# A metaformer of four blocks on one core: another order in attention and triangle, shorter batch statistics, and half of a scan's centring ahead of a verdict

## The reference, cut to what matters

```
x = x + L0_conv(_ln_c(x))      # linear attention: softmax(q), softmax(k), context = k^T v
t = t + L0_ffn(_ln_t(t))       # spectral filters (STU): a causal convolution over 256 tokens
x = x + L1_conv(_ln_c(x))      # triangle: a, b = sigmoid products of x; z = a * b; g * (ln(z) Wz + bz)
t = t + L1_ffn(_ln_t(t))       # recurrence with batch statistics of Wx
x = x + L2_conv(_ln_c(x))      # scan over 16 image rows: row + relu(conv(previous row))
t = t + L2_ffn(_ln_t(t))       # 16 experts, top 8 tokens each
x = x + L3_conv(_ln_c(x))      # the same scan again, with other weights
t = t + L3_ffn(_ln_t(t))       # the same recurrence again

# L1_ffn and L3_ffn
mean, var = jnp.mean(flat, axis=0), jnp.var(flat, axis=0)     # flat = W x, over all 32 * 256 tokens
Wx = (flat - mean) * rsqrt(var + 1e-5) * gamma + beta
y[t] = sigmoid(Wx[t] + y[t-1] @ V.T)                           # 256 steps
```

## Time and profile before

| | |
|---|---|
| median of 3 runs | 474.16 us (472.72 to 477.4) |
| profiled execution | 474.01 us, span 471.9 us |
| TensorE busy | 424.3 us (90%), 2880 matmul passes |
| VectorE busy | 246.3 us (52%) |
| ScalarE busy | 181.3 us (38%) |
| GpSimd busy | 32.9 us (7%) |
| granted TensorE clock, mean | 0.975 |

### The profile page before, as it was taken

The page is one execution under the profiler, slowest core; times in us unless marked ns, Lnnn a source line. Parts: engine busy times, 40 slices in busy tenths (PEclk is TensorE's granted clock), DMA queues, the critical chain, the costliest instruction groups (busy, mean ns, idle before and its releaser), DMA issues.

```text
span 471.9 us, 7130 instructions
## 1 busy us (share of the span) xinstructions
PE 424.3 (90%) x2880; PEld 260.1 (55%) x2880; DVE 246.3 (52%) x486; ACT 181.3 (38%) x373; POOL 32.9 (7%) x39
## 2 busy tenths in 40 slices
PE   6967999999879999998999999897999899999990
PEld 2434656554255567653765555394475474475590
DVE  3499677786778050106103746646534628434735
ACT  1776777755530002001102643454504631414360
POOL 0037222222000000000000000000000000000000
PEclk8898999999999999999999999998999999999997
DMA  9940000079940000000002000000000000000003
GB/s 222 135 97 1 1 1 1 2 160 219 203 90 0 1 0 0 1 0 0 1 0 47 0 1 3 0 1 2 0 1 2 2 0 1 0 1 1 0 1 90
DMA packets 6479, 15.24 MB, mean 32 GB/s; under 512 B 2718, under 2 KB 5422, under 8 KB 5806
## 3 DMA queue, kind: packets, MB, share of 16 engines
q1 hardware_dynamic: 5870, 14.25, 14.9%
q10 hardware_dynamic: 576, 0.52, 0.3%
HBM read 5.86 MB, written 1.05 MB: 15 GB/s over the span
## 4 chain that ended last, share of the span: by engine, by line
PE 66%; DVE 17%; ACT 10%; issue 3%; DMA 1%; POOL 1%; POOLq 0%; SPq 0%; DVEq 0%; ACTq 0%
PE bank L673 20%; PE bank L532 17%; PE bank L213 6%; PE bank L861 5%; PE bank L207 4%; PE bank L806 4%; PE bank L817 3%; PE bank L229 2%; ACT lnv L272 2%; ACT rs L277 2%; DVE xn L259 1%; DVE xQ L1294 1%; DMA xR<-in_x 1%; PE bank L605 1%; ACT arena L1019 1%
## 5 line engine op out<-in xcount | busy, mean ns | idle before, releaser
L673 PE MATMUL bank<-xn,arena 128*128 128x512 f32 (+15 forms) x332 | 88.9, 427 | 2.4 <-DVE xn L259 2.4
L673 PEld LDWEIGHTS bank<-xn,arena 128*128 128x128 f32 x332 | 56.3, 190 | 36.0 <-issue 27.0
L266 ACT ACTIVATE sq<-bank 128x512 f32<-128x512 f32 x36 | 21.3, 591 | 118.0 <-PE bank L207 98.3
L532 PE MATMUL bank<-sb_consts 128*128 128x512 f32 (+1 forms) x116 | 52.9, 569 | 1.6 <-ACT arena L1153 1.6
L532 PE MATMUL bank<-xn,sb_w_attn 128*128 128x512 f32 x64 | 35.4, 644 | 4.8 <-ACT attn_scratch L990 3.7
L213 PE MATMUL bank<-sq,sb_consts 128*128 128x512 f32 x72 | 38.7, 623 | 0.7
L272 ACT ACTIVATE lnv<-bank 128x512 f32<-128x512 f32 x36 | 21.5, 597 | 35.4 <-PE bank L213 35.3
L1303 DVE TENSOR_TENSOR arena<-bank,rs 128x512 f32<-128x512 f32 x4 | 4.2, 1038 | 51.4 <-ACT rs L277 51.4
L532 PEld LDWEIGHTS bank<-sb_consts 128*128 128x128 f32 x116 | 20.5, 194 | 18.7 <-issue 16.5
L861 PEld LDWEIGHTS bank<-arena,sb_w_late 128*128 128x128 f32 x180 | 23.0, 191 | 11.1 <-DVE arena L1470 8.0
L861 PE MATMUL bank<-arena,sb_w_late 128*128 128x128 f32 x180 | 27.2, 287 | 1.7 <-DVE arena L1470 1.3
(11 more groups left out here) (193 smaller groups left out, 623.5 us busy)
## 6 DMA issues: line engine op xcount, KB each, us to landing
arena<-arena SPq DMA_DIRECT2D x4, 1024.0 KB, 16.0
arena<-arena SPq DMA_DIRECT2D x4, 512.0 KB, 8.7
arena<-in_w_spec SPq DMA_DIRECT2D x2, 720.0 KB
sb_w_late<-in_w_late SPq DMA_DIRECT2D x1, 1100.5 KB, 22.8
xR<-in_x SPq DMA_DIRECT2D x4, 256.0 KB, 4.5
arena<-arena SPq DMA_DIRECT2D x4, 256.0 KB, 4.1
sb_w_attn<-in_w_attn SPq DMA_DIRECT2D x1, 641.0 KB, 7.4
arena<-in_w_spec SPq DMA_DIRECT2D x2, 256.0 KB
```

What stands on the lines that cost most here:

```text
L266: act.activation(sq[:, i % 2, :], bank[:, centre_bank(i), :], ACT.Square).then_inc(S("ln_squared"), 1)
L532: return mm(ps, lhsT, rhs, start=True, stop=True)
L673: return mm(bank[:, k, lo * B:hi * B], lhs, cols[:, at * B:(at + hi - lo) * B], start=start, stop=stop, **kw)
```

## The change

It has four parts, and all of the diff is in them.

1. Attention: on TensorE the query product, the first filter and the value products of a turn move behind the transposes of the unit before (`attn_q_v`). On ScalarE a turn now begins with the query exponential and the key copy of the unit before, then the key exponentials, then the copy of the first filter; the query exponential of a unit thus moves to the next turn.
2. Triangle: the a-product's slices are given out in fours between the last steps of the spectral stage (`a_columns`), three of four in place of filler products; VectorE adds the bias to the first half of them ahead of the last normalisation; ScalarE makes two of its three scaled copies ahead of the sigmoids of b; the two numbers of fillers go from 3 and 4 to 2 and 2.
3. Batch statistics: two one-column operations are folded into their neighbours, one copy leaves the path, and one copy goes, ScalarE reading the bank itself. The shift of the scaling is now formed with the other sign.
4. First scan: `ln_centre_r` takes a set of residues. For quarters 0 and 1 the products r = 2, 3 run inside `rnn(0)`, the first two behind the sixth early state and ahead of the verdict's product, the second two in place of a filler; the products r = 0, 1 follow at the scan's start and wait for the eighth state instead of for GpSimd's release. Bank 3 takes the verdict's sum instead of bank 0.

The core of the diff:

```diff
-BUSY_ATTN, BUSY_TRI, BUSY_SCAN, BUSY_LOGITS = 4, (3, 4, 6, 1), 3, 2
+BUSY_ATTN, BUSY_TRI, BUSY_SCAN, BUSY_LOGITS = 4, (2, 2, 6, 1), 3, 2
-ACT_BD = 3
+ACT_BD, ACT_BD_FIRST = 3, 2
+LATE_R = (2, 3)
...
-                for m in filter_turn(u, 0):
-                    filters(m)
+
+            def attn_q_v(u):
+                j, q = divmod(u, NQ)
                 if u >= 1:
                     pe.wait_ge(S("q_shift"), u)
                 full(bank[:, 2, :], wq[:, q, :], flat(xn, j)).then_inc(S("q_ps"), 1)
+                for m in filter_turn(u, 0):
+                    filters(m)
...
                 if 0 <= i - 1 < U:
                     attn_mid(i - 1)
+                if i < U:
+                    attn_q_v(i)
...
-            keep_busy(BUSY_STU, 6)
+            def a_columns(ms):
+                for m in ms:
+                    pe.wait_ge(S("ln_applied"), 3 * CH + m // 4 + 1)
+                    last = full(bank[:, m // 4, (m % 4) * P:(m % 4 + 1) * P],
+                                xnH[:, m, :, :].rearrange("p g w -> p (g w)"), wa)
+                    if m % 8 == 7:
+                        last.then_inc(S("ab_ps"), 1)
...
-                pe.wait_ge(S("bn_v"), i + 1)
+                pe.wait_ge(S("bn_rstd"), i + 1)
...
+                if i == 0:
+                    pe.wait_ge(S("x_early"), RES - 2)
+                    ln_centre_r(pe, CH * (k + 1), xsQ, LATE_R)
                 pe.wait_ge(S("settled_rows"), i + 1)
-                full(bank[0:1, 0, 0:1], moved[:, 1:2], ones[:, 0:1]).then_inc(S("settled_sum"), 1)
+                full(bank[0:1, 3, 0:1], moved[:, 1:2], ones[:, 0:1]).then_inc(S("settled_sum"), 1)
                 if i == 0:
-                    keep_busy(BUSY[5], 4)
+                    ln_centre_r(pe, CH * (k + 1) + 1, xsQ, LATE_R)
...
-                    ln_pe_r(pe, k, xsQ, lambda: pe.wait_ge(S("x_rnn0"), 1))
+                    ln_pe_r(pe, k, xsQ, lambda: pe.wait_ge(S("x_early"), RES), (0, 1))
...
+                if 0 <= i - 1 < U:
+                    a_q(i - 1)
+                    a_kn(i - 1)
+                if i < U:
+                    a_k(i)
                 for m in filter_turn(i, 0):
                     a_filters(m)
-                if i < U:
-                    a_k(i)
                 if i == 0:
                     ln_rstd(act, 3)
-                if 0 <= i - 1 < U:
-                    a_kn(i - 1)
                 if i < U:
                     a_v(i)
-                    a_q(i)
...
+            act.wait_ge(S("a_s"), 1)
+            blocks_of_a(range(ACT_BD_FIRST))
             act.wait_ge(S("b_in"), 1)
...
-                act.wait_ge(S("bn_v"), i + 1)
-                link(act.activation(rst[:, 5:6], rst[:, 10:11], ACT.Ln, bias=LN_TOK))
+                act.wait_ge(S("bn_var"), i + 1)
+                link(act.activation(rst[:, 5:6], bank[:, 5, 0:1], ACT.Ln, bias=LN_TOK))
...
+            dve.wait_ge(S("w_late_in"), 16)
+            link(add_ab_bias(0, 0))
             normalise(3)
...
+                link(dve.tensor_tensor(rst[:, 1:2], mv[:, 0:1], bank[:, 4, 0:1], ALU.subtract))
+                dve.scalar_tensor_tensor(out=rst[:, 2:3], in0=rst[:, 1:2], scalar=rst[:, 1:2], in1=mv[:, 1:2],
+                                         op0=ALU.mult, op1=ALU.add).then_inc(S("bn_var_in"), 1)
                 link(dve.tensor_copy(rst[:, 0:1], bank[:, 4, 0:1]))
-                link(dve.tensor_tensor(rst[:, 1:2], mv[:, 0:1], rst[:, 0:1], ALU.subtract))
-                link(dve.tensor_tensor(rst[:, 3:4], rst[:, 1:2], rst[:, 1:2], ALU.mult))
-                dve.tensor_tensor(rst[:, 2:3], rst[:, 3:4], mv[:, 1:2], ALU.add).then_inc(S("bn_var_in"), 1)
-                dve.wait_ge(S("bn_var"), i + 1)
-                dve.tensor_copy(rst[:, 10:11], bank[:, 5, 0:1]).then_inc(S("bn_v"), 1)
                 dve.wait_ge(S("bn_rstd"), i + 1)
                 link(dve.tensor_tensor(rst[:, 7:8], rst[:, 6:7], rgam[i], ALU.mult))
-                link(dve.tensor_tensor(rst[:, 8:9], rst[:, 7:8], rst[:, 0:1], ALU.mult))
-                link(dve.tensor_tensor(rst[:, 9:10], rbet[i], rst[:, 8:9], ALU.subtract))
+                link(dve.scalar_tensor_tensor(out=rst[:, 9:10], in0=rst[:, 7:8], scalar=rst[:, 0:1], in1=rbet[i],
+                                              op0=ALU.mult, op1=ALU.subtract))
```

More of the change, by code:

```diff
@@ L244, in centre_of @@
                 else:
[L245 removed]
+                    ln_centre_r(pe, i, s, rs_)
             ln_pe(pe, k, lambda q: src, ready_at, centre_of)
@@ L1075, in _ @@
             last.then_inc(S("b_s"), 1)
[L1076 to L1080 removed]
+            blocks_of_a(range(ACT_BD_FIRST, ACT_BD)).then_inc(S("a_bd"), 1)
             act.wait_ge(S("gate_ps"), 1)
@@ L1328, in _ @@
                     dve.wait_ge(S("a_in"), 1)
-                pre4 = ab_pre.rearrange("p (m n) -> p m n", n=2 * CT)
-                for half in range(2):
-                    dve.wait_ge(S("ab_ps"), 2 * k + half + 1)
-                    first = 4 * k + 2 * half
-                    last = dve.tensor_tensor(pre4[:, 32 * half:32 * half + 32, :],
-                                             bank[:, first:first + 2, :].rearrange("p k (m n) -> p (k m) n", n=2 * CT),
-                                             ab_bias[:, k:k + 1, :].to_broadcast([P, 32, 2 * CT]), ALU.add)
+                    link(add_ab_bias(1, 0))
+                last = add_ab_bias(k, 1)
                 last.then_inc(S(["a_pre", "b_pre"][k]), 1)
```

55 lines of the change are left out of this document (32 added, 23 removed).

## The result

| | median us | runs | lowest to highest |
|---|---|---|---|
| before, beside the first measurement | 473.44 | 4 | 472.65 to 477.4 |
| changed kernel | 467.11 | 4 | 464.85 to 469.42 |

A forecast was written before the change was run, and what follows sets the result against it. The prediction took one long chain to bound the kernel, TensorE having 66% of the span. Attention -1.0, triangle -4.2, batch statistics -0.95 and first scan -1.45 sum to -7.6, from 474.0 to 466.4 us; range 463.2 to 470.3.

The forecast's parts named there:

- late start: Attention: ScalarE's later query exponentials delay the first filter by 3.3 to 4.0 us, taken as 3.6.
- 1.5 + 3.2: Attention: 1.5 us returns as query product and transposes precede the first filter; 3.2 us from ScalarE waits shed in the loop.
- at no cost since VectorE decides there: Attention, 36 to 38 us: the kernel before has its clock at 1.2 GHz, said to cost nothing.
- the steps folded: Batch statistics: two folded steps and a copy off the path save 0.39 us, of which the filler lets 0.1 show.
- the sum by rows: Batch statistics: by the profile, reading the product's bank costs nothing more, giving -0.95; the Trainium skill's table would give -0.8.
- The two other terms: Batch statistics: ScalarE reading the product itself saves 0.17 us, one step fewer behind the exponential 0.19.
- half of 3.80 us is left for after it [...] and needs 1.9 us: First scan: with half the centring of quarters 0 and 1 before the verdict, TensorE needs 1.9 us after it.
- the wait for strips: First scan: TensorE would wait for VectorE's strips before quarter 3, the strips being the new bound; term -1.45 us.
- Rival 4: Slower: longer idle before unit 3 carries 1.2 GHz clock into the filter loop; 20 us gives 476.4 us; chance 0.04.
- Rival 1: Attention: the filters' late start does not come, attention -4.5 us, total 462.9 us; chance 0.12.
- rival 2: Attention costs 3 us: filter copies still end last or the start is later still; total 470.4 us; chance 0.12.
- rival 3: First scan gives nothing, since the strips or GpSimd's release decide; total 467.9 us; chance 0.12.

The follow-up runs named there:

- the last version of experiment 4: Changed kernel with ScalarE's attention order as before, no filler in the batch statistics, and the spectral stage's two idle times filled: median 462.84 us, ratio 0.975 to before.
- experiment 2: Changed kernel with both moved copies of a behind b's sigmoids again: spectral stage's end to first of the 64 products 22.65 us (changed 20.87, before 25.07).
- experiment 1: Kernel before with the whole attention edit (474.52 us), only TensorE's order (attention stretch 100.95 us), or only ScalarE's order (496.98 us).
- three groups ahead: Changed kernel with three of four column groups of both quarters centred ahead of the verdict: strips' copies to last normalisation 10.07 us, squares 1.13 us apart.

## Why the prediction was right, and where it was not

- *Attention, -1.0 forecast (the sum's own -1.1, rounded), -1.31 measured in these two profiles.* The terms: late start 3.6 forecast, 3.4 in the head (30.86 - 27.49); of the rest 1.5 + 3.2 = 4.7 forecast, 4.68 in the loop. Signs named beforehand: first filter near 50.5 (50.31), no ScalarE wait in the loop (none), key product of unit 13 about 1 us earlier (92.34, 1.23 earlier), 5.25 us per unit (5.33). The two versions with ScalarE's old order and full clock there have a head of 26.77, and the last version of experiment 4, which has a spell there, 27.40, so 0.6 to 0.7 of the 27.49 was most likely the low clock of the earlier trace rows: "at no cost since VectorE decides there" was not quite right. Part of the agreement is luck. Of the eight profiles with the whole attention edit, four have 105.0 to 105.3 us in this stretch and four 106.3 to 106.4, as the kernel before's one profile. In three of the latter a spell begins at 49.3 to 49.5 us, just behind the first filter, and the loop takes 72.2 to 72.4 us instead of 71.08.
- *Triangle, -4.2 forecast, -4.20 measured*, with ScalarE's third copy last as forecast; experiment 2 splits it.
- *Batch statistics, -0.95 forecast, -0.98 measured.* 0.1 of the steps folded shows and the filler hides the rest, as argued. The step that reads the product's bank takes 0.16, and the sum by rows stood. The two other terms were off and made up for each other: from the variance product to ScalarE's logarithm 0.30 went instead of 0.17, for the product itself became 0.1 shorter, and from the exponential to the first scaling 0.06 (0.82 to 0.76) instead of 0.19, for the folded step takes 0.22 and VectorE starts 0.07 later behind the exponential.
- *First scan, -1.45 forecast, -0.83 measured. This term failed.* The step was "half of 3.80 us is left for after it [...] and needs 1.9 us". Dividing a time by the share of the passes left assumed that they run one after the other. They run side by side in four column groups, and the passes of each group decide; the half needed 3.7 us, ScalarE's chain behind the second square and not VectorE's strips stayed the bound, and the wait for strips forecast as a sign did not come. What gain there was came from a line that the prediction had read as the start of the work only: TensorE no longer waits for GpSimd's release (0.6 to 0.8); the halves themselves gave about 0.05.
- *The clock, nothing forecast, +3.24 in the profiled execution.* Rival 4 had lower clock as its mechanism, at another place: in the filter loop. This profile shows none there; three of the eight with the whole attention edit do, at a cost of 1.2 to 1.3 us and not 10. Without the two spells the profiled span would be 464.4 and the execution 466.2. The four runs of the first measurement follow their mean granted clock: 0.968, 0.973, 0.976 and 0.980 for 469.42, 467.71, 466.5 and 464.85 us. The medians gained 6.3 us in the first measurement and 5.1 in the second, against the 6.6 to 7.3 that the edits' own stretches sum to. Filling the gaps gave 2.8 back, so the changed kernel most likely loses to these two places in most runs. Whether it meets them more often than the kernel before did stays open: that kernel and its three variants of experiment 1 show none, one, one and one, the changed kernel and its variants with unfilled gaps from none to two.
- *Rivals.* Rival 1 (no late start) and rival 2 (the loop's waits stay) are excluded by head and loop; rival 3 (no gain in the scan) was wrong as well, but named the release, which decided. The total, 0.7 us off the first median and 2.6 off the second, is thus the sum of a triangle that went as argued, a scan that gave 0.6 less, batch terms that made up for each other, and a clock that differs from run to run.

## What to carry to other kernels

Before a product is split or moved in part, its passes' lengths should be added and held against the time of the group: where the sum is a multiple of the group's time, they overlap, and leaving out half of them may save nothing. What counts here is how many passes each column group still has. An edit that reorders two engines is two edits; here one of them gave the whole gain and the other cost 3.4 to 4.1 us, which only a run of each alone showed. Idle times of TensorE that cost nothing by themselves can still be worth a filler, if it ends ahead of the wait.

## What the runs showed of the hardware that was not expected

- 128x512 passes into 32 partitions each: sixteen of 1.08 us in 3.80 us, eight of them in 3.7 to 3.8. Passes of one column group follow each other by 0.89 to 0.91 us, whether one, two or four groups work.
- With three groups ahead, a pass of a later product started before two of an earlier one in another group (321.46 against 322.10 and 323.00), but ScalarE was let go only when the earlier one was over (324.08, square at 324.13).
- After an idle time of 2.3 to 2.4 us the granted clock fell to its 1.2 GHz level in some executions and not in others, at the same place and length; each spell cost 1.65 us in the spectral stage, and with two filler products at each place none was seen in two profiles (of the twelve without them three have none either).
- A one-column product takes 0.28 us where its weight loads start 0.24 us ahead of it behind a filler (300.97 and 301.21), and 0.38 where the first load and the product start together, be it after an idle time (295.52 and 295.53 without the filler) or not (303.78 and 303.79 in the kernel before).
